# A graph layer's dense edge pairs: one comparison per unit, y rows stationary in the sums, 15 dense blocks with 21 gathered groups, and the first slot lists loaded ahead of the last table

## The reference

```python
for _ in range(3):                                   # first layer: three hops
    msg = (x * norm_out[:, None])[src]
    agg = segment_sum(msg, dst, num_segments=N)
    x = 0.5 * (agg * norm_in[:, None]) + 0.5 * h0
y = layernorm(h0 + x @ W.T)
h = relu(concat([y[src], y[dst]]) @ W1 + b1)         # second layer: a weight for each edge
w = sigmoid(h @ W2 + b2)[:, 0]
agg = segment_sum(w[:, None] * y[src], dst, num_segments=N)
out = layernorm(y + layernorm(y + agg) * gamma + beta)
```

## Time and profile before

| | |
|---|---|
| median of 3 runs | 1135.87 us (1132.98 to 1136.27) |
| profiled execution, its own time | 1132.37 us |
| span of the profiled execution, first to last instruction | 1130.4 us |
| mean granted TensorE clock | 0.95 of full speed |
| busy share of the span | PE 85%, DVE 85%, ACT 54%, POOL 53% |
| chain of work that ended last, by engine | DVE 34%, POOL 28%, issue 16%, PE 15% |

### The profile page before, as it was taken

How to read it: one execution, slowest core, us unless ns; L and a number is a source line. 1 busy time by engine, 2 the same in 40 slices (tenths; PEclk the granted TensorE clock), 3 DMA queues, 4 the chain that set the end, 5 groups by cost and what they waited for, 6 DMA issues and landing times.

```text
span 1130.4 us, 33410 instructions
## 1 busy us (share of the span) xinstructions
PE 962.6 (85%) x11292; PEld 803.4 (71%) x11293; DVE 966.1 (85%) x2583; ACT 607.6 (54%) x1511; POOL 599.0 (53%) x742
## 2 busy tenths in 40 slices
PE   4889889788889998889569999999899989999850
PEld 2888888577678886778447788888677767777740
DVE  7999999699999998778459999999788878888766
ACT  6666766511100001222158787888677767777665
POOL 1000000347664533666677777777777777777711
PEclk9999999899989999999779999999999999999985
DMA  3000000000000000111277677777777677677601
GB/s 102 2 1 0 0 0 0 1 1 2 2 3 3 3 3 13 37 33 51 63 231 206 207 219 211 224 205 227 191 212 209 205 212 204 200 213 207 189 17 49
DMA packets 77516, 117.44 MB, mean 104 GB/s; under 512 B 20488, under 2 KB 38972, under 8 KB 77372
## 3 DMA queue, kind: packets, MB, share of 16 engines
q1 hardware_dynamic: 58172, 63.13, 18.7%
q0 software_dynamic: 19200, 52.45, 16.8%
HBM read 108.66 MB, written 6.86 MB: 102 GB/s over the span
## 4 chain that ended last, share of the span: by engine, by line
DVE 34%; POOL 28%; issue 16%; PE 15%; ACT 4%; DMA 1%; SPq 1%; DVEq 1%; ACTq 0%; POOLq 0%
POOL region L934 18%; POOL U L934 7%; PE bank L1787 6%; DVE stage L1040 4%; DVE hx L1040 3%; DVE aggT L1223 3%; POOL stage L934 2%; DVE stage L1203 2%; DVE stage L1216 2%; DVE aggT L1040 2%; PE bank L1748 1%; DVE stage L1212 1%; DVE U L1274 1%; DVE t L1291 1%; ACT region L2015 1%
## 5 line engine op out<-in xcount | busy, mean ns | idle before, releaser
L934 POOL DMA_INDIRECT region<-src_split,region x272 | 264.7, 973 | 84.4 <-issue 81.9
L1787 PE MATMUL bank<-U,region 128*128 128x256 f16 (+1 forms) x1875 | 241.5, 280 | 5.9 <-DVE U L1307 3.1
L1787 PEld LDWEIGHTS bank<-U,region 128*128 128x128 fp8e4 x1875 | 182.6, 100 | 41.0 <-DVE U L1307 3.6
L2173 ACT CAST region<-bank 128x512 f16<-128x512 f32 x338 | 180.8, 593 | 0.0
L2051 ACT CAST region<-bank 128x500 f32 x202 | 119.9, 593 | 55.4 <-PE bank L1676 46.5
L2153 ACT ACTIVATE region<-bank 128x512 f16<-128x512 f32 x169 | 100.9, 597 | 60.4 <-PE bank L1887 55.8
L1464 DVE SCALAR_TENSOR_TENSOR region<-bank,region 128x512 f16<-128x512 f32 x169 | 116.3, 688 | 11.5 <-ACT region L2153 8.2
L823 POOL TENSOR_TENSOR aggT<-stage 128x520 f16<-128x520 f16 x52 | 76.2, 1485 | 92.9 <-DVE stage L1200 87.7
L1884 PE MATMUL bank<-region,xs 128*128 128x256 f16 x676 | 104.2, 277 | 19.1 <-DVE region L1464 12.1
L1448 DVE TENSOR_SCALAR region<-region,stage 128x512 f16<-128x512 f16 x338 | 109.2, 364 | 9.8 <-DMA region<-slot_rows 9.8
L934 POOL DMA_INDIRECT U<-src_split,region x96 | 93.3, 972 | 29.3 <-issue 29.3
(11 more groups left out here) (295 smaller groups left out, 2386.7 us busy)
## 6 DMA issues: line engine op xcount, KB each, us to landing
region<-slot_rows SPq DMA_DIRECT2D x169, 256.0 KB
region<-in_dst_dram SPq DMA_DIRECT2D x100, 64.0 KB
region<-src_split,region POOLq DMA_INDIRECT x272
slot_rows<-aggT SPq DMA_DIRECT2D x104, 3.2 KB
src_split<-U SPq DMA_DIRECT2D x25, 64.0 KB, 1.5
src_split<-xs SPq DMA_DIRECT2D x25, 64.0 KB, 1.5
tgt_split<-q SPq DMA_DIRECT2D x25, 64.0 KB, 1.6
region<-tgt_split SPq DMA_DIRECT2D x100, 16.0 KB
```

Source lines behind the costliest of these rows:

```text
L934: nc.gpsimd.indirect_dma_start(out=rows_of(n, i), out_offset=None, in_=src_split, in_offset=bass.IndirectOffsetOnAxis(ap=listed[n % LISTS] ...
L1787: z = nc.tensor.matmul(bank[2 * (k % 2) + p][:, 0:width], count[:, h, b * P:(b + 1) * P], U[k % 2][:, h, 0:width], start=h == 0, stop=h == ...
L2173: nc.scalar.copy(y_rows[u % 4][:, a, :], bank[3 + a][:, :]).then_inc(rows_copied, 1)
```

## The change

Numbers: `POOLED` goes from 25 to 21 groups and `FIRST_BLOCK` from 12 to 10, so `DENSE` goes from 13 to 15 blocks, the units from 169 to 195, and the half blocks to sort from 26 to 30. The indirect gathers go from 400 to 336.

Lists: a unit's lists now lie in DRAM twice, once for the lower and once for the upper 64 partitions, so that the target lists of the upper half hold the target's number less an offset. So a half block is stored by 8 DMAs and not 4, two of them from a new tile `upper_targets`, of which there is one. ACT writes that tile just ahead of the copy of the lists, and waits before it until all stores of the earlier half blocks have landed. A unit's lists are loaded by two DMAs of 64 partitions, and one comparison of 1024 columns takes the place of two of 512.

Sums: the y rows are the stationary operand and the weights the moving one: 8 matmuls of 128 and 64 columns by turns take the place of 4 of 256. The fold of a block is 2 matmuls and not 4, from half as many columns.

Start of the second layer: DVE no longer waits for the last block's P and Q, the first three loads of lists stand ahead of the last table's stores on SP, the first units wait for their own source blocks only, and the loads of windows are issued in halves.

```diff
-    POOLED = 25
+    POOLED = 21
-    FIRST_BLOCK = 12
+    FIRST_BLOCK = 10
+    STORED = 16 * 8
...
             def load_slots(u):
                 i, m = divmod(u, UNITS)
                 if u >= 3:
                     sp.wait_ge(turned_ready, u - 2)
+                for h in range(2):
+                    sp.dma_start(slots_here[u % 3][h * HD:(h + 1) * HD, :],
+                                 slot_rows[i, m:m + 1, h, :].broadcast_to([HD, 8 * P])).then_inc(slots_loaded[u % 3], 16)
...
+            def first_loads():
+                sp.wait_ge(hop_psum, 3 * NB)
+                sp.wait_ge(q_tabled[FIRST_BLOCK % 2], 16 * (FIRST_BLOCK // 2 + 1))
+                sp.wait_ge(slots_stored, STORED * HALF_BLOCKS)
+                load_slots(0)
+                targets_of(0)
+                load_slots(1)
+                load_slots(2)
...
             def store_slots(hs):
                 i, t = divmod(hs, 2)
                 sp.wait_ge(slots_copied, hs + 1)
+                for k in range(2):
+                    first, at = 64 * t + (2 + k) * UNITS, (2 * k + t) * P
+                    for h in range(2):
+                        sp.dma_start(slot_rows[i, :, h, at:at + P], turned_slots[i][first:first + UNITS, :])\
+                          .then_inc(slots_stored, 16)
+                    first, at = 64 * t + k * UNITS, (4 + 2 * k + t) * P
+                    for h, lists in enumerate((turned_slots[i], upper_targets)):
+                        sp.dma_start(slot_rows[i, :, h, at:at + P], lists[first:first + UNITS, :])\
                           .then_inc(slots_stored, 16)
...
             for c in range(NB + 2):
+                if c == NB + 1:
+                    first_loads()
                 tables(c, c % 2)
...
-            dve.wait_ge(pq_split, NB)
             dve.wait_ge(slots_ready, HALF_BLOCKS)
...
             def turn_pair(u):
-                dve.wait_ge(slots_loaded[u % 3], 16 * (u // 3 + 1))
+                dve.wait_ge(slots_loaded[u % 3], 32 * (u // 3 + 1))
...
-                for a in range(2):
-                    z = nc.vector.tensor_scalar(turned_hot[u % 3][:, a * 4 * P:(a + 1) * 4 * P],
-                                                slots_here[u % 3][:, a * 4 * P:(a + 1) * 4 * P],
-                                                row_no[:, a:a + 1], None, ALU.is_equal)
-                z.then_inc(turned_ready, 1)
+                nc.vector.tensor_scalar(turned_hot[u % 3][:, :], slots_here[u % 3][:, :], row_no[:, 0:1], None,
+                                        ALU.is_equal).then_inc(turned_ready, 1)
...
                     for t in range(2):
-                        z = nc.tensor.matmul(
-                            bank[7][:, t * 2 * D:(t + 1) * 2 * D],
-                            hot_weights[u % 3][:, 2 * i:2 * i + 2, :, t].rearrange("p a r -> p (a r)"),
-                            y_rows[u % 4][:, i, t * 2 * D:(t + 1) * 2 * D],
...
+                        for y_half in range(2):
+                            z = nc.tensor.matmul(
+                                bank[7][:, t * P:t * P + (2 - y_half) * HD],
+                                y_rows[u % 4][:, i, (2 * t + y_half) * D:(2 * t + y_half + 1) * D],
+                                hot_weights[u % 3][:, 2 * i:2 * i + 2 - y_half, :, t],
...
             def copy_lists(hs, s):
                 i, t = divmod(hs, 2)
                 act.wait_ge(slots_psum, hs + 1)
-                nc.scalar.copy(turned_slots[i][64 * t:64 * t + 2 * BUCKETS, :],
-                               bank[7 if s < 2 * NB else 3][0:2 * BUCKETS, 0:P]).then_inc(slots_copied, 1)
+                here = bank[7 if s < 2 * NB else 3]
+                if hs:
+                    act.wait_ge(slots_stored, STORED * hs)
+                nc.scalar.activation(upper_targets[64 * t:64 * t + BUCKETS, :], here[0:BUCKETS, 0:P], ACT.Identity,
+                                     bias=half_offset[0:BUCKETS, 0:1])
+                nc.scalar.copy(turned_slots[i][64 * t:64 * t + 2 * BUCKETS, :], here[0:2 * BUCKETS, 0:P])\
+                  .then_inc(slots_copied, 1)
```

More of the change, by code:

```diff
@@ L182, in gnn_kernel @@
         ohT = [carve(region, taken, [BE], f16) for _ in range(2)]
-        qwin = [carve(region, taken, [2 * D], f16) for _ in range(2)]
+        qwin = [sb(f"qwin{i}", [P, 2 * D], f16) for i in range(2)]
         ohJ = [carve(region, taken, [TPS // 2, JW, 2], f16) for _ in range(2)]
@@ L670, in _, with window_half @@
                 sp.wait_ge(q_tabled[p], 16 * ((NB + 1 - p) // 2))
[L673 to L681, removed]
+            window_first = [None]
+            def window_half(n, p, half):
+                if half == 0:
+                    if n >= 2:
+                        sp.wait_ge(ohT_ready, n - 1)
+                        sp.wait_ge(s_psum, (n - 1) * BPS)
+                    window_first[0] = load_four(ET.SP, base[0], n, N)
+                for q in range(half * BPS // 2, (half + 1) * BPS // 2):
+                    sp.dma_start(qwin[p][q * QR:(q + 1) * QR, :], tgt_split[bass.ds(window_first[0][q], QR), :])\
                       .then_inc(win_loaded[p], 16)
-                for q in range(BPS):
                     at = n * (BPS * BE) + q * BE
@@ L687, in window @@
                                  .broadcast_to([QR, BE])).then_inc(win_loaded[p], 16)
[L688 to L706, removed]
             for s in range(STEPS):
                 b = batch_at[s]
-                if s + 1 < TOTAL:
+                if 2 < s + 1 < TOTAL:
                     load_slots(s + 1)
[L711 to L714, removed]
-                    window(b // BPS + 1, (b // BPS + 1) % 2)
+                if 2 <= s < 6:
+                    window_half((s - 2) // 2, (s - 2) // 2, s % 2)
+                if b is not None and b % BPS < 2 and 2 <= b // BPS + 1 < POOLED:
+                    window_half(b // BPS + 1, (b // BPS + 1) % 2, b % BPS)
                 i = due(s, UNITS - 7, UNITS, DENSE - 1)
@@ L827, in judge @@
             def judge(part):
-                link = chained(g, "keys", 6 + 2 * part, 2)
+                link = chained(g, "keys", 5 + 2 * part, 2)
                 if part == 0:
@@ L1917, in fold_parts @@
                 pe.wait_ge(parts_copied, i + 1)
[L1918 to L1922 removed]
+                for part in range(2):
+                    z = nc.tensor.matmul(bank[2][:, P:2 * P], att_parts[:, part, :, :].rearrange("p t r -> p (t r)"), ident[:, :],
+                                         start=part == 0, stop=part == 1)
                 z.then_inc(parts_folded, 1)
```

79 lines of the change are left out of this document (41 added, 38 removed).

## The result

The changed kernel takes 1236.31 us (median of 4 runs, 1235.41 to 1237.54) against 1136.07 before: a ratio of 1.0889, 95% interval 1.0866 to 1.0911. It is slower, as forecast, but by 100 us and not by 54, and outside the range of 1150 to 1222. The span of the profiled execution grows from 1130.4 to 1234.8 us.

What follows compares the result with a forecast made beforehand. It took PE and DVE, nearly full, to bound hops 0 and 1, and a three-engine ring, with gathers close, the loop. 12 + 38 − 9.6 + 14 = +54 gave 1190 us, range 1150 to 1222.

Steps and rivals of the forecast that it cites:

- A: Hops 0 and 1: 2.7 more half blocks of sorting at DVE's price of 4.5 us each, +12 us.
- B: Hop 2: ACT's copy of lists waits until the earlier half block's stores have landed, +38 us, bounds +22 and +75.
- the chain: Hop 2: copy, node, y, tables, stores and next copy follow serially, taken at 15 us from copy to copy.
- 41 less 3: Hop 2: 8 × (15 − 9.9) = 41 us, less 3 because the last copy finds PE half a step further on.
- the neighbour's 1.6: Hop 2: a neighbouring store's landing of 1.6 us, used for the lists' stores, whose landing the trace lacked.
- C: Start of the second layer: earlier list loads −4.1 us, shorter first to fourth unit −5.5, together −9.6.
- D: Second layer's loop, fourth to last unit: from 499.2 to 513.2 us, +14, bounds −7 and +32.
- the sum before its savings: Loop: 192 × 2.32 for units, 84 × 0.70 for batches and about 20 more, 524.2 us before 8 and 3 come off.
- the rest: Loop: window comparisons, folds and y plus beta, 23.3 us before and about 20 after.
- The hidden wait: Hop 2: ACT's wait for stores is hidden, leaving 4 us of PE work; sum +20, time 1156, chance 0.18.
- the gathers alone: Loop: gathers alone set its length, so it shrinks from 511 to 430 us; time 1109, chance 0.05.
- The long chain: Hop 2: copy to copy takes 19.2 us all through, +75 there, sum +91; time 1227, chance 0.11.

Runs made afterwards that it cites:

- e13: The kernel of e3_parity with the old two numbers (25 groups, 13 dense blocks): 1145.62 us, ratio 1.0093.
- e14: The kernel of e13 with the first loads of lists behind the last table's stores: 1140.45 us, ratio 1.0038.
- e1_numbers: The kernel before with the two new numbers alone (21 groups, 15 dense blocks, 30 half blocks): 1217.05 us, ratio 1.0725.
- e3_parity: The changed kernel, but ACT waits only for the stores that last used its half of the tile: 1201.96 us, ratio 1.0579.
- e5_late: The kernel of e3_parity with PE's count moved from the middle to the end of its step: 1170.19 us, ratio 1.0289.
- e4_lag3: The changed kernel with DVE's places made in step s + 3, not s + 4, so no step holds three parts: 1239.37 us, ratio 1.0905.
- e2_edits: The changed kernel with the old two numbers (25 groups, 13 dense blocks, 26 half blocks): 1171.29 us, ratio 1.0311.
- e10_mixed: The kernel of e5_late with 23 groups and 14 dense blocks, the count late in hops 0 and 1 alone: 1133.39 us, ratio 0.9987.
- e8_oldsum: The kernel of e3_parity with the old sums and fold of the kernel before: 1213.54 us, ratio 1.0693.
- e9_twocmp: The kernel of e3_parity with two comparisons of 512 columns a unit in place of one of 1024: 1208.0 us, ratio 1.0644.

## Why the prediction missed

**What bounds the kernel.** "both are nearly full, and what is added to DVE's sort work there lengthens the hops" gave the right sign. But the sum took the hops for one engine's stream of work, and left out that the two engines also wait for each other in turn within a step. Of the loop it said that the gather "ends last now and then, and not always". With 25 groups that was too weak: e13 and e14 show that the end moves with the first gather. With 21 groups it is true that it does not bind (the last unit at 1190.2, the last gather at 1153.8).

**A, the step that failed.** "One half block costs DVE ... 4.5 us" and "2.7 × 4.5 = +12 us" priced DVE's work and put the waiting that this work causes at nothing: PE's count waits for DVE's scan in the middle of PE's step, and the fill, the rest of the step and with it DVE's next step stand behind it. The work itself was priced well. DVE's six sort operations take 97.3 us in hops 0 and 1 before and 109.8 after, 12.5 more:

```profile
L1234 DVE TENSOR_TENSOR aggT<-twice,stage 128x2560 f16<-128x2560 f16 x20 | 30.3, 1517 | 0.3
L1214 DVE TENSOR_TENSOR_SCAN stage<-stage 128x520 f16<-128x520 f16 x21 | 26.1, 1241 | 0.7
L1227 DVE TENSOR_REDUCE stage<-stage 128x20 f16<-128x520 f16 x20 | 21.4, 1072 | 0.7
L1223 DVE TENSOR_TENSOR stage<-stage,bank 128x520 f16<-128x520 f16 x20 | 13.8, 688 | 0.1
L1225 DVE TENSOR_TENSOR stage<-stage 128x520 f16<-128x520 f16 x20 | 9.2, 459 | 0.7
L1211 DVE TENSOR_TENSOR stage<-stage 128x520 f16<-128x520 f16 x21 | 9.0, 428 | 0.6
```

The runs put in place of +12: +48 to +51 from the numbers alone (after, e1_numbers), with PE's wait at the count 49.7 us and not 10.7, and 37.5 us that go when the count is moved behind the step's matmuls (e3_parity to e5_late). Nor did the prediction ask how many parts fall into the same step; that they do is part of the cause, shown for 12 us (e4_lag3).

**B, right in mechanism, short in size.** Ten waits of ACT in hop 2 that SP's DMAs end, 53.3 us in all, the longest 10.2 where 4 to 9 were forecast; the granted clock falls. The mis-sized term is the chain: taken at 15 us from copy to copy, it measured 16.8 as a mean over the eight distances of two steps (14.7 to 18.8). In the prediction's own sum that is 8 × (16.8 − 9.9) = 55 of the 58 us by which hop 2 grew, in place of its 41 less 3. The chain is as long with 26 half blocks (17.0 over three distances in e2_edits), so the added half blocks do hide in the waits, as the prediction said. They show when the wait is taken out: two steps then take 12.2 us with 30 half blocks (e3_parity) and 9.9 with 26 (e13_early13), and hop 2 stays 17 to 20 us above the kernel before (e1_numbers, e3_parity). So it is chance that the wait taken out saves 38.2 us (after less e3_parity), just the number forecast: the chain was longer than forecast, and so was what it is measured against. With 26 half blocks it saves 24.7 (153.7 in e2_edits, 129.0 in e13_early13). Why the added half blocks lengthen hop 2 by as much as 20 us was not settled; the place of the count is not it (e10_mixed). The landing of a list's store, 1.4 us from its issue to ACT, is near the neighbour's 1.6. The Trainium skill's 2.0 ("DMA: Bandwidth & Descriptors", Anatomy of one DMA) is given there for DMAs that GpSimd issues; these stores are SP's, and this trace shows less for them.

**C, half right, and then lost.** The first `pair_rest` comes 3.0 us sooner (17.9 behind the hops, not 20.9), the fourth unit 5.6. By the eleventh nothing is left: 52.2 us behind the hops against 52.0 before. In its place DVE waits nine times for lists while SP issues the windows' halves between them (655 to 712 us after; in 548 to 605 before it was 9.8 us in 3):

```profile
DVE region L1457 <- DMA region<-slot_rows: 16.7, 9, 4.4
...
POOL region L945 <- DMA src_split<-xs: 5.1, 1, 5.1
```

The second row is what the prediction did not look for: the first gather waits for the table's stores that the loads were moved past.

**D, right in sign, 8 us too high.** Steps without a batch stay at 2.32 us (median), steps with one come to 2.93, where "about 2.9" was said, and PE has no wait for gathered rows. The single comparison, bounded by 0.36 and 0.61 and taken at 0.5, measured 0.522. The sums save 12 us, not 8, and the comparison 6, not 3, each taken alone against e3_parity, since both also shorten some steps without a batch, where they were said to gain nothing. But the 8 us do not come from there. With neither edit, e1_numbers has a loop of 513.6 us where the sum before its savings had 524.2: of the term "the rest", taken at 20, some 12 are there (513.6 − 191 × 2.32 − 84 × 0.70; from the fourth unit to the last are 191 steps, not 192). All edits together then gain 8 us (after) to 10 (e3_parity), near the 11 forecast, though partly by chance: 14 are gained from the eleventh unit on, and 4 lost before it, as told under C. The ending behind the last unit is 4.1 us shorter, which was not in the sum; e1_numbers has it too (44.5), so it belongs to the numbers.

**The rivals.** The hidden wait (1156) is refuted by ACT's row; the gathers alone (1109) by a loop that gets longer with fewer gathers. The long chain gave nearly the right time, 1227, for the wrong reason: the chain was 16.8, not 19.2, and the rest stood in hops 0 and 1.

## What to carry to other kernels

The price of added work on one engine is the price in time only while no other engine stands waiting for it in the middle of its own step. Before pricing, look in the trace for such a wait between two in-order engines, even a small one (here 10.7 us before), and list what stands behind it in both queues: the place of one short matmul within its step was worth 37.5 us. Where work is laid over steps by a rule, list also which parts meet in one step; here that was worth 12. A wait for a store costs what stands ahead of that store on its queue, so move the store or the wait before adding buffers. And before moving loads ahead on a queue, look for who waits for what they pass.

## What the runs showed of the hardware

Eight matmuls of 128 and 64 columns by turns pass through PE in less time than four of 256, though their listed busy times add up to more (8 × 206 ns against 4 × 274 ns). A unit's sums in the changed kernel and in the kernel before:

```profile
903.27 0.51 PE L1920 MATMUL bank<-region 128*128 128x128 f16 x8
```

```profile
602.26 0.60 PE L1909 MATMUL bank<-region 128*128 128x256 f16 x4
```

Over all units the stretches are 0.51 and 0.60 us as a mean. By the busy times the new sums would have cost 0.55 us more a unit; e8_oldsum shows that they save. For matmuls that overlap, the stretch of a run of them is to be read, not the sum.

The same holds for DVE's comparisons. One over 1024 columns takes 522 ns as a mean and one over 512 takes 364. But two of 512 in a row do not take 728 ns: as a pair, from the first start to the last end, they take 646 ns as a mean in the kernel before and 638 in e9_twocmp. So the single comparison saves DVE some 0.12 us a unit, and not the 0.2 that the busy times give. All of them in the changed kernel, then one pair in e9_twocmp:

```profile
L1457 DVE TENSOR_SCALAR region<-region,stage 128x1024 f16<-128x1024 f16 x195 | 101.7, 522 | 16.7 <-DMA region<-slot_rows 16.7
```

```profile
901.05 0.61 DVE L1461 TENSOR_SCALAR region<-region,stage 128x512 f16<-128x512 f16 x2
```
